# Regrouping one sequence's tail: two recurrence units move from the attention steps to the experts, with new orders on every engine

## What is computed

```
xn = layernorm(x)
# recurrence: 16 heads of 16x16 state, one step per token
r, k, v, g, w = low-rank mixes of xn and its predecessor, each projected by a 256x256 matrix
st = w * st + k^T v ;  y = r (st + u k^T v)
s  = (silu(g) * layernorm16(y)) @ oW.T
# gate: attention block and mixture of experts
z  = xn + attention(rmsnorm(xn))            # 16 heads of 64, causal, latent keys and values
zn = rmsnorm(z)
f  = z + expert_shared(zn) + sum over the best 2 of 8 experts of p_e * expert_e(zn)
out = x + s * silu(f)
```

## Time and profile before

| what | value |
|---|---|
| median of 3 runs | 2258.83 us (2255.39 to 2259.88) |
| profiled execution, its own time | 2257.5 us |
| its span, first to last instruction | 2255.7 us |
| mean granted clock of TensorE, share of full | 0.957 |
| busy: PE / DVE / ACT / POOL | 91% / 78% / 43% / 37% of the span |
| one sequence of the second layer, step 0 to step 0 | 208.2 us (830.4 to 1038.6) |

### The profile page before, as it was taken

One profiled execution on the slowest core, in us unless ns is written; L12 is line 12 of the kernel. 1 busy time (PEld: TensorE's weight loads), 2 busy tenths in 40 slices (PEclk: granted clock), 3 DMA queues, 4 the chain that ended last, 5 costly groups with the idle time before them and its releaser, 6 DMA issues.

```text
span 2255.7 us, 37286 instructions
## 1 busy us (share of the span) xinstructions
PE 2057.1 (91%) x11722; PEld 1245.7 (55%) x11723; DVE 1758.3 (78%) x2906; ACT 976.9 (43%) x2556; POOL 836.6 (37%) x666
## 2 busy tenths in 40 slices
PE   7998599998998999999899989998998999899887
PEld 4554499997455445544554555455455545554553
DVE  5997466664598879778886988798789869887985
ACT  2544244442375247234623651373247236623731
POOL 1335200001443354435334542643354335336421
PEclk9999799998899999999999999999999999999998
DMA  6554422113213013211221220122022211211310
GB/s 173 148 151 143 148 54 56 55 53 100 76 55 83 10 51 78 70 38 43 67 52 42 61 84 11 44 80 76 22 54 67 56 43 53 65 40 42 77 51 10
DMA packets 145727, 151.18 MB, mean 67 GB/s; under 512 B 47664, under 2 KB 105648, under 8 KB 145584
## 3 DMA queue, kind: packets, MB, share of 16 engines
q1 hardware_dynamic: 138288, 136.73, 22.3%
q0 software_dynamic: 3072, 8.41, 1.2%
q10 hardware_dynamic: 4224, 4.19, 0.7%
HBM read 121.71 MB, written 27.43 MB: 66 GB/s over the span
## 4 chain that ended last, share of the span: by engine, by line
PE 33%; issue 20%; DVE 13%; POOL 7%; ACT 3%; DMA 0%; POOLq 0%; DVEq 0%; ACTq 0%
PE bank L1379 11%; PE bank L1238 5%; PE bank L1255 4%; PE bank L1292 3%; POOL arena L2063 3%; PE bank L1392 3%; DVE arena L1778 2%; ACT arena L1584 2%; DVE arena L1791 2%; PE bank L1265 2%; PE bank L1171 2%; DVE arena L1798 2%; PE bank L1241 1%; DVE arena L2005 1%; POOL arena L2055 1%
## 5 line engine op out<-in xcount | busy, mean ns | idle before, releaser
L2055 POOL TENSOR_TENSOR arena<-arena 128x512 f32<-128x512 f32 x256 | 354.8, 1387 | 586.4 <-DVE arena L1798 560.2
L1379 PE MATMUL bank<-arena 128*128 128x512 f32 (+2 forms) x1312 | 442.7, 492 | 6.8 <-DVE arena L1923 6.8
L1171 PE MATMUL bank<-arena 128*128 128x512 f32 (+2 forms) x768 | 361.1, 617 | 24.3 <-DVE arena L1722 17.9
L1379 PEld LDWEIGHTS bank<-arena 128*128 128x128 f32 x1312 | 254.3, 208 | 179.9 <-issue 148.9
L1798 DVE TENSOR_TENSOR_SCAN arena<-arena 128x512 f32<-128x512 f32 x256 | 350.0, 1367 | 1.8
L1584 ACT ACTIVATE arena<-bank,arena 128x128 f32<-128x128 f32 (+3 forms) x512 | 266.1, 529 | 191.8 <-DVE arena L1778 191.8
L1791 DVE TENSOR_TENSOR arena<-arena 128x512 f32<-128x512 f32 x256 | 239.5, 936 | 39.8 <-DMA arena<-values 27.2
L1171 PEld LDWEIGHTS bank<-arena 128*128 128x128 f32 (+2 forms) x768 | 141.0, 191 | 217.9 <-issue 175.1
L1238 PE MATMUL bank<-arena 64*128 64x128 f32 (+3 forms) x1024 | 208.8, 484 | 55.3 <-ACT arena L1584 52.0
L1778 DVE TENSOR_REDUCE arena<-bank 128x2 f32<-128x256 f32 (+3 forms) x256 | 207.2, 810 | 23.4 <-PE bank L1241 22.9
L1593 ACT ACTIVATE arena<-bank 128x128 f32<-128x128 f32 (+3 forms) x512 | 196.1, 438 | 39.5 <-PE bank L1255 39.0
(11 more groups left out here) (200 smaller groups left out, 2906.6 us busy)
## 6 DMA issues: line engine op xcount, KB each, us to landing
arena<-values SPq DMA_DIRECT2D x256, 256.0 KB, 3.5
arena<-in_L_attn_h SPq DMA_DIRECT2D x16, 512.0 KB, 4.8
arena<-in_W1T SPq DMA_DIRECT2D x8, 1024.0 KB, 5.1
arena<-in_W2T SPq DMA_DIRECT2D x8, 1024.0 KB, 9.0
sorted_rows<-arena SPq DMA_DIRECT2D x42, 128.5 KB, 10.5
arena<-sorted_rows SPq DMA_DIRECT2D x40, 128.5 KB, 2.1
arena<-in_b2row SPq DMA_DIRECT2D x40, 128.0 KB, 3.0
gate_rows<-arena SPq DMA_DIRECT2D x39, 128.0 KB, 1.7
```

Of the source, the lines that this page charges most:

```text
L1171: last = nc.tensor.matmul(dst[rows, :], w, x, start=(n == 0), stop=(n == len(pairs) - 1))
L1379: last = nc.tensor.matmul(dst[o], w, x, start=first, stop=last_one)
L2055: nc.gpsimd.tensor_tensor(prods[(n + 2) % PRODS], state[n % STATES][:, 0:T], proj["r"][:, m, :], ALU.mult).then_inc(prod_done, 1)
```

## The change

- `STEPPED` goes from 20 to 18 and `EARLY` from 22 to 20: units 2 to 17 are in the steps, with two parts in steps 16 and 24 only. The tail handles units 18 to 20. Units 21 to 31 are in the experts, by the table `EXPERT_UNITS`; 21 comes right after the routing. `reduce_state` 5, 6, 7 come at experts 3, 6, 8 (before 2, 4, 8), and `reduce_state` 4 moves from the middle of the output projection to behind the first turned rows.
- The turned rows are made and brought back in halves (`xc00` to `xc11`). Between the halves PE makes `reduce_state` 4, `var0`, half of the logits and the first half (256 columns) of `g0` and `u0`.
- DVE goes from the turned rows and one scan straight into the routing; `hidden(0)` comes before the routing's last operations. On ACT `g0`'s silu comes first.
- The head of the next sequence is normalised by ACT (`norm_head`: scale and bias) in place of DVE; DVE makes the shift and the mean square from the variance (`head_shift`, four operations on 128x4). The squares with accumulation on ACT (`square_head`) are gone. `head_lerp` moves from `between(7)` to `between(6)`, and in `between` each head part but `head_shift` and `head_lerp` stands before the units.
- `ln_inv`, `ln_scale` and `ln_gate` of the first half move, except for the last sequence, into the next `before_attention`, behind the first four blends. The silu of the accumulated rows moves there too. The third low-rank product `la_d` comes before `mean_last`.
- The last expert is added in two operations of 128x512 instead of four of 128x256.
- Banks of PSUM are dealt out anew. SP's list of transfers is unchanged. On POOL the gather now comes after product 22.

```diff
-EARLY = 22
-STEPPED = 20
+EARLY = 20
+STEPPED = 18
+EXPERT_UNITS = {0: (22, 23), 1: (24, 25), 2: (26,), 3: (27,), 4: (28, 29), 5: (30, 31)}
+REDUCED = ((3, 5), (6, 6), (ME, 7))
...
-        n = 2 if i % NT == 0 and i > NT else 1
+        n = 2 if i % GSTEPS == 0 and i > GSTEPS else 1
...
-                reduce_state(b, STEPPED // 4 - 1)
                 pe.wait_ge(y_out, GROUPS * b + GROUPS)
...
+                turn_rows(0)
+                reduce_state(b, 4)
+                pe.wait_ge(sq_done, 2 * b + 1)
+                result(b, "var0", [(full, mean_m, sq[0], True, True)], bank[post.bank("var0")])
+                pe.wait_ge(v_read2, post.read(b, "xc00"))
+                pe.wait_ge(a_read2, post.read(b, "xc01"))
+                pe.wait_ge(moe_in, 16 * 3 * (ME + 1))
+                begin(b, "gate", post, post_read)
+                gate_tiles(0)
+                first = (("g0", eg_w[0]), ("u0", eu_w[0]))
+                for name, w in first:
+                    begin(b, name, post, post_read)
+                    up_half(name, w, 0)
+                turn_rows(1)
+                pe.wait_ge(v_read2, post.read(b, "xc10"))
+                pe.wait_ge(a_read2, post.read(b, "xc11"))
+                gate_tiles(1).then_inc(made2, 1)
+                for name, w in first:
+                    up_half(name, w, 1).then_inc(made2, 1)
...
+            def norm_head(b):
+                if b:
+                    act.wait_ge(v_read2, post.read(b - 1, "d0b"))
+                act.wait_ge(shift_done, b + 1)
+                for i in range(NT):
+                    last = nc.scalar.activation(xn[:, i, :], s_in[:, i, :], ACT.Identity, scale=rstd[:, i:i + 1], bias=shift[:, i:i + 1])
+                last.then_inc(xn_done, 1)
...
                 def between(e):
-                    if e == 0:
-                        unit(b, EARLY + 3)
-                    if e < 6:
-                        unit(b, EARLY + 4 + e)
+                    if not final:
+                        if e == 1:
+                            head_gate(b + 1)
+                        elif e == 2:
+                            head_sum(b + 1)
+                        elif e == 3:
+                            head_stats(b + 1)
+                    for n in EXPERT_UNITS.get(e, ()):
+                        unit(b, n)
+                    if not final:
+                        if e == 4:
+                            head_shift(b + 1)
+                        elif e == 6:
+                            head_lerp(b + 1)
...
             def experts(b, final):
-                product(b, EARLY + 1)
-                product(b, EARLY + 2)
+                for n in range(EARLY + 1, EXPERT_UNITS[0][-1]):
+                    product(b, n)
                 if not final:
                     g.wait_ge(pv_mm, CHUNKS * b + 2 * CHUNKS)
                     gather(b + 1)
-                for n in range(EARLY + 3, UNITS):
-                    if n == UNITS - 2 and not final:
-                        head_rstd(b + 1)
-                    product(b, n)
-                if not final:
-                    head_rms(b + 1)
+                for n in range(EXPERT_UNITS[0][-1], UNITS):
+                    product(b, n)
+                    if n == EXPERT_UNITS[3][-1] and not final:
+                        head_rstd(b + 1)
+                    if n == EXPERT_UNITS[4][-1] and not final:
+                        head_rms(b + 1)
```

More of the change, by code:

```diff
@@ L1018, in phase_c @@
         waste = mem.take(NT)
+        shift, msq = mem.take(NT), mem.take(NT)
         eps_d, root = mem.take(NT), mem.take(NT)
@@ L1412, in attention @@
                         spread_inverse(b, (i - GSTEPS - 4) // GSTEPS)
-                    for g in range(STEPPED // 4 - 1):
+                    for g in range(4):
                         if i == UNIT_STEP[4 * g + 3] + 3:
@@ L1430, in experts, with turn_rows @@
             def experts(b, final):
-                for k in range(KD):
-                    begin(b, f"xc{k}", post, post_read)
-                for half in range(2):
+                def turn_rows(half):
+                    for k in range(KD):
+                        begin(b, f"xc{half}{k}", post, post_read)
                     pe.wait_ge(xc_done, 2 * b + half + 1)
@@ L1436, in experts @@
                         for i in (2 * half, 2 * half + 1):
[L1437 to L1442, removed]
+                            last = nc.tensor.transpose(bank[post.bank(f"xc{half}{k}")][:, (i % 2) * P:(i % 2 + 1) * P],
+                                                       xb[:, i, k * P:(k + 1) * P], ident)
@@ new lines, in turn_rows, with gate_tiles, up_half @@
+                    last.then_inc(made2, 2)
+                def gate_tiles(half):
+                    dst = bank[post.bank("gate")]
+                    for i in (2 * half, 2 * half + 1):
+                        for k in range(KD):
+                            last = nc.tensor.matmul(dst[:, i * ME:(i + 1) * ME], xbT[:, k, i * P:(i + 1) * P], gate_w[:, k, :],
+                                                    start=(k == 0), stop=(k == KD - 1))
+                    return last
+                def up_half(name, w, half):
+                    cols = slice(2 * P * half, 2 * P * (half + 1))
+                    for k in range(KD):
+                        last = nc.tensor.matmul(bank[post.bank(name)][:, cols], w[:, k, :], xbT[:, k, cols],
+                                                start=(k == 0), stop=(k == KD - 1))
+                    return last
@@ L1546, in take2, with silu_rows @@
                 return nc.scalar.activation(dst, bank[post.bank(name)][:, :], func, **kw)
+            def silu_rows(b):
+                act.wait_ge(v_read2, post.read(b, f"d{ME}b"))
+                nc.scalar.activation(acc, acc, ACT.Silu).then_inc(f_done, 1)
             def root_last(b):
@@ L1560, in before_attention @@
                 if ended is not None:
+                    silu_rows(ended)
                     root_last(ended)
@@ L1655, in experts @@
                     scale_head(b + 1)
-                act.wait_ge(v_read2, post.read(b, f"d{ME}b"))
-                nc.scalar.activation(acc, acc, ACT.Silu).then_inc(f_done, 1)
                 if final:
+                    silu_rows(b)
                     root_last(b)
@@ L1731, in _ @@
             head_stats(0)
-            head_norm(0)
-            head_ms(0)
+            head_shift(0)
             head_lerp(0)
@@ L1830, in before_attention @@
                     center_last(ended)
-                for name in ("v0", "k0", "v1", "k1", "d0", "d1", "r0", "g0", "r1", "g1"):
+                for name in ("v0", "k0", "v1", "k1"):
                     blend(name)
                 if ended is not None:
+                    ln_inv(ended, 0)
+                for name in ("d0", "d1", "r0", "g0", "r1", "g1"):
+                    blend(name)
+                if ended is not None:
+                    ln_scale(ended, 0)
+                    ln_gate(ended, 0)
                     ln_inv(ended, 1)
@@ L1983, in between @@
                         ln_scale(b, 0)
-                    elif e == 8:
                         ln_gate(b, 0)
+                    if e == ME:
                         read_out(b, 1)
-                    for at, part in ((1, head_gate), (2, head_sum), (3, head_stats), (4, head_norm), (6, head_ms), (7, head_lerp)):
-                        if e == at and not final:
-                            part(b + 1)
-                hidden(0)
+                outer(b, EARLY + 1)
+                for n in range(EARLY + 1, EXPERT_UNITS[0][0]):
+                    unit(b, n)
                 for e in range(ME + 1):
```

104 lines of the change are left out of this document (56 added, 48 removed).

## The result

The changed kernel takes 2234.04 us (median of 5 runs, 2231.31 to 2235.81), the kernel before 2255.39 (median of 5, 2249.27 to 2259.88). The ratio is 0.9905, with an interval of 0.9883 to 0.9927: faster by 21 us, where 42 were forecast. The forecast time of 2217 was counted from the 2258.83 known then; 2234.04 lies 17 above it. The profiled execution took 2231.31 us, its span is 2229.5.

What follows compares the result with a forecast made beforehand. DVE bounds the attention steps, PE the experts and what follows. A middle sequence: -3.7 + 1.5 - 2.1 = -4.3 us; seven give -30, the last -11.7, -42 in all: 2217 us, own range 2198 to 2238, eight in ten 2190 to 2256.

Steps and rivals of the forecast that it cites:

- Attention steps: Four parts leave the steps (8, 12, 20, 28); three of them save 1.24 us each, 3.7 us per sequence.
- Tail: Tail of attention: moved work fills PE's wait, the logits' second half comes 1.5 us earlier, and the half clock goes.
- The new wait: In between(1), head_gate waits about 9.5 us for the load of s, behind product 23 and the gather.
- T': The start of the second half of the logits, from which the forecast times the experts; forecast at 923.1.
- a unit is 1.9 net of overlap, so 7.7: DVE from head_gate to expert 7's accumulation: four more units add 7.7 us, within a sum of 35.0.
- rival C: POOL's products hold DVE up in the eight units behind the stall; 1.2 us each gives 2284; chance 0.13.
- Before attention: From the experts' end on: no PE hole or half clock, la_d covers the tanh wait; net -2.1 us.
- Last sequence: It loads nothing, so no wait: -3.7, -1.5, -4.1 clock and -2.4 moved work, together -11.7 us.
- Rival A: The loads come in time without a stall, each of seven sequences another 12 us shorter, about 2133; chance 0.08.
- Rival B: The steps do not get shorter, since PE and the exponentials take over; about 2247; chance 0.12.
- rival D: Half clock after the new wait in the experts; 26 us per sequence if it stayed throughout, 2257 + 140; chance 0.07.

Runs made afterwards that it cites:

- e1_both: The changed kernel with SP's loads after copy 24 instead of 28 and POOL's gather before product 21: 2167.43 us, ratio 0.9621 to the kernel before.
- e2_gather: The changed kernel with only POOL's gather moved, from behind product 22 to ahead of product 21: 2201.82 us, ratio 0.9773 to the kernel before.
- e3_load: The changed kernel with only SP's loads moved, after copy 24 instead of 28: 2198.35 us, ratio 0.9749 to the kernel before.
- e4_split: e1_both with the two units of experts 0, 1, 4 and 5 pulled apart around the accumulation: 2144.26 us, ratio 0.9509 to the kernel before.
- e8_shift_first: e4_split with head_shift at the front of between(4) and POOL's head_rstd ahead of product 27: 2136.22 us, ratio 0.9477 to the kernel before.
- e9_lerp_and_norm: Kernel before, head_lerp behind expert 6; first half's reciprocal, scale, gate in the next before_attention, except for the last sequence: 2228.95 us, ratio 0.9888.
- e6_lerp_early: The kernel before with head_lerp and the reciprocal changing places in between: 2249.29 us, ratio 0.9976.

## Why the prediction was right in its sign, and the gain half of what it said

- **Attention steps: right, a little more.** 3.7 us forecast, 4.4 measured (67.6 to 63.2). The four parts took more than their own time with them: the mean outer fell from 1.12 us to 0.94, so DVE's busy time fell by 7.0 us, not 4.9. PE, busy for 60.0 of 63.2 us, leaves little more to win there.
- **Tail: right.** 1.5 us forecast; from step 31 to the logits' second half it takes 1099.4 to 1119.3 = 19.9 us instead of 903.1 to 924.6 = 21.5. No half clock follows there.
- **The new wait: right**, in place, cause and size (9.5 us forecast, 10.5 measured, seven times; the load lands at T' + 27.9 instead of 27.5), and `e1_both`, `e2_gather` and `e3_load` show its two causes apart.
- **The term of the sum that was too small: "a unit is 1.9 net of overlap, so 7.7", with `head_shift` at 0.5.** The stretch from `head_gate` to the last accumulation was forecast at 35.0 us and took 1185.2 - 1147.2 = 38.0. A single unit takes 1.8 us, but two in a row take 1152.91 - 1148.34 = 4.6, since the second scan runs beside the first one's product; the change has three such pairs there (the last, with one outer less, takes 3.8) where the kernel before had none. The eight units took 16.5 us against 6.5 for four before, that is 10.0 for four more instead of 7.7, and `head_shift` took 1.6 instead of 0.5. `e4_split` and `e8_shift_first` show that it is the product beside them that does it. This was rival C in small, at 0.4 us per unit with `head_shift`'s share in it, where it would have turned the sign at 0.75. The price of a pair could be read ahead of any run, from units 25 and 26 in the kernel before: 944.66 - 940.09 = 4.6 us. The 1.40 of the earlier trace rows is the mean of this long scan and six short ones, and the change adds pairs:

```profile
940.09 1.28 DVE L1798 TENSOR_TENSOR_SCAN arena<-arena 128x512 f32<-128x512 f32 x1
941.28 0.67 DVE L1791 TENSOR_TENSOR arena<-arena 128x512 f32<-128x512 f32 x1
941.98 2.17 DVE L1798 TENSOR_TENSOR_SCAN arena<-arena 128x512 f32<-128x512 f32 x1
944.08 0.66 DVE L1791 TENSOR_TENSOR arena<-arena 128x512 f32<-128x512 f32 x1
944.66 0.67 DVE L1973 TENSOR_TENSOR arena<-arena,bank 128x512 f32<-128x512 f32 x1
```

- **Before attention: right.** 2.1 us forecast, 54.4 to 52.1 measured. `e9_lerp_and_norm` shows the hole and its half clock alone; `la_d` ahead of `mean_last` was not run by itself.
- **Last sequence: right.** 11.7 us forecast; from its step 0 to the end 164.6 us against 177.1, 12.5 less. That is about half of the whole gain: the seven other sequences, which wait for their loads, give about as much together.
- Rival A did not occur in the change; the kernel that makes it true takes 2167, not 2133, for DVE and not PE bounds its experts (55.8 us from T' instead of 50.5). Rival B is ruled out by the 63.2 us. Of rival D, the half clock does come twice, behind both new holes (1139.7 to 1146.6 at 0.51, and 3.4 us from 1153.4), but PE waits for DVE by 0.48 us once more before the end, so it is DVE's length that counts; the half clock was hidden, as said.

The stretches add up: this sequence takes 206.5 us (1031.1 to 1237.6), against 208.2 before: -4.4 - 1.6 + 6.6 - 2.3 = -1.7. The forecast had -4.3. The stretch from T' to the low-rank product is 3.6 us longer than it said (66.2 for 62.6), 3.0 of them by the term above and 0.4 by the later landing; the steps, the tail and what follows the experts gave 1.0 back. Seven times the 2.6 that are left, less the 0.8 more in the last sequence, are the 17 us above 2217. That the time still lies in the forecast's own range of 2198 to 2238 is luck in part: its width was drawn from the stall and the steps, which came out as said, and not from the term that erred.

What stays open: why a hole sometimes is followed by half clock and sometimes not (below); how much of the gain of `e4_split` is due to the order of `head_gate` and unit 24 rather than to the shorter scans; and where the 8 us between the medians of `e4_split` and `e8_shift_first` lie, of which the profiled executions show 1.2.

## What to carry to other kernels

When work moves later on one engine, list what other queues have hung on it: a transfer that was issued 20 us ahead of its use because it followed the 23rd product becomes a 10 us wait when the 23rd product moves, without a line of the transfer's code changed. Give loads for the next round their own early place, ahead of anything that waits for compute. Before two pieces of one kind are put side by side, look in the trace for such a pair: a mean over single pieces does not price it. A move between two stages is worth the difference between what the work costs in the two: here it was worth -29, 2 or 23 us, by what bounded the experts.

## What the hardware showed that I had not expected

- Some operations of DVE stand still until the POOL operation beside them has ended, however small they are. `head_shift`'s first operation, on 128x4 elements, starts at 1170.60 and ends at 1171.82, the product beside it at 1171.80; alone it takes 148 ns. A scan that meets a product ends 1.1 us after it: at 1152.41 behind 1151.33 in the changed kernel, at 1129.45 behind 1128.36 in `e8_shift_first`; so it takes 1.5 to 2.2 us instead of 1.28. These all have two inputs in SBUF. The accumulation with one operand in PSUM kept its 1.65 us for four beside the product of 1152.48, and the reduction L2000, with its one input in SBUF, its 0.19 beside the product of 1120.47. The Trainium skill, "SBUF — State Buffer" (two separate sides), states the lock for DVE operations with two inputs in SBUF; these rows agree, and show it for the scan too.
- The half clock does not follow the length of the hole in a simple way. A hole of 3.27 us was followed by 10.2 us at 0.50. One of 4.77 had 6.9 us at 0.51 from 1.0 us before its end, one of 3.67 was followed by 3.4 us. In `e6_lerp_early` PE idles 2.38 us before L1303, and the matmuls behind it run at full clock, while 2.55 us before L1171 were followed by 3.3 us at 0.50. In `e1_both` the very same hole in two sequences ends both ways: the matmuls behind it take 7.02 us once, with a half clock among them (0.62 on average from 953.0 to 956.5), and 5.33 the other time, at full clock:

```profile
951.12 1.09 PE L1301 MATMUL bank<-arena 128*128 128x128 f32 x8 [2.67 <-ACT arena L1535]
952.05 7.02 PE L1382 MATMUL bank<-arena 128*128 128x256 f32 x16
...
1148.15 1.09 PE L1301 MATMUL bank<-arena 128*128 128x128 f32 x8 [2.67 <-ACT arena L1535]
1149.08 5.33 PE L1382 MATMUL bank<-arena 128*128 128x256 f32 x16
```
- With two units fewer in the steps, the remaining work of DVE and POOL there is shorter too: the mean outer went from 1124 to 943 ns, and POOL's mean operation from 1.39 us (30.53 for 22) to 1.33 (26.65 for 20). That they meet each other less often is the likely reason; no run tests it there.
